# Routing turns moved from TensorE to VectorE, and routing products gathered into seven visits

## The reference

```python
h = einsum('bsd,bdh->bsh', x, W[cat]) + b[cat][:, None, :]      # 4096 x 512
probs = softmax(h @ Wr, axis=-1)                                # 8 experts
eidx = argmax(probs, axis=-1); p_tok = probs[eidx]
rank = cumsum(onehot(eidx)) - onehot(eidx)   # place in the expert's queue
keep = rank < 512                            # capacity 4096 / 8
xe = h[dispatch]                             # 8 x 512 x 512
ye = relu(xe @ W1) @ W2                      # hidden width 2048
out = x + scatter(ye * p_tok * keep)
```

## Time and profile before

| | us |
|---|---|
| median of three runs | 802.54 |
| lowest and highest | 802.49, 803.22 |
| span of the profiled execution (first to last instruction) | 800.5 |
| TensorE busy in it | 792.1 (99%) |
| VectorE busy | 576.6 (72%) |
| GpSimd busy | 512.8 (64%) |
| ScalarE busy | 351.4 (44%) |
| granted TensorE clock, mean | 0.999 of full |

### The profile page before, as it was taken

How to read it: one execution, slowest core, us unless ns; L and a number is a source line. 1 busy time by engine, 2 the same in 40 slices (tenths; PEclk the granted TensorE clock), 3 DMA queues, 4 the chain that set the end, 5 groups by cost and what they waited for, 6 DMA issues and landing times.

```text
span 800.5 us, 14226 instructions
## 1 busy us (share of the span) xinstructions
PE 792.1 (99%) x5267; PEld 704.0 (88%) x5267; DVE 576.6 (72%) x760; ACT 351.4 (44%) x537; POOL 512.8 (64%) x392
## 2 busy tenths in 40 slices
PE   9999999999999999999999999999999999999997
PEld 6788889899999999999999999999999999999996
DVE  5677878778767896589657965786578866895532
ACT  4322337445444544445444644464445444554430
POOL 1000148866888688787887688768876888663601
PEclk9999999999999999999999999999999999999999
DMA  8987545541544255524543454435541544255201
GB/s 279 371 300 274 226 128 183 184 134 59 189 160 145 103 180 174 170 105 170 166 155 130 161 167 144 157 102 171 176 146 55 194 152 155 104 183 178 71 1 53
DMA packets 61102, 127.20 MB, mean 159 GB/s; under 512 B 8310, under 2 KB 8310, under 8 KB 60562
## 3 DMA queue, kind: packets, MB, share of 16 engines
q1 hardware_dynamic: 47714, 95.19, 34.2%
q0 software_dynamic: 13216, 31.38, 12.1%
q10 hardware_dynamic: 144, 0.26, 0.1%
HBM read 110.13 MB, written 25.17 MB: 169 GB/s over the span
## 4 chain that ended last, share of the span: by engine, by line
PE 94%; DVE 3%; issue 1%; DMA 1%; ACT 1%; POOL 1%; POOLq 0%; ACTq 0%
PE y_ps L1502 44%; PE acc_ps L1403 20%; PE tp_ps L1403 19%; PE acc_ps L1311 5%; PE tp_ps L1311 2%; PE tp_ps L1237 1%; PE acc_ps L1329 1%; DMA early_rows<-h_rows,tok_all 1%; PE acc_ps L1295 1%; PE y_ps L1217 0%; POOL early_rows L532 0%; DVE x_split L1044 0%; DVE w_split L949 0%; DVE rows L863 0%; DVE first_x_sums L1048 0%
## 5 line engine op out<-in xcount | busy, mean ns | idle before, releaser
L1502 PE MATMUL y_ps<-w_split,xt_split 128*128 128x512 f32 x1536 | 371.2, 391 | 0.8 <-issue 0.8
L1502 PEld LDWEIGHTS y_ps<-w_split,xt_split 128*128 128x128 f32 x1536 | 280.7, 188 | 54.3 <-issue 1.0
L1403 PE MATMUL acc_ps<-x_split,w_split 128*128 128x256 f32 x1320 | 180.9, 283 | 0.8 <-DVE w_split L949 0.8
L960 DVE TENSOR_TENSOR w_split<-stage,w_split 128x1024 fp32r<-128x1024 f32 x64 | 115.7, 1846 | 90.6 <-ACT w_split L669 90.6
L1403 PEld LDWEIGHTS acc_ps<-x_split,w_split 128*128 128x128 f32 x1320 | 172.0, 191 | 5.7 <-DVE w_split L949 1.0
L1403 PE MATMUL tp_ps<-x_split,w_split 128*128 128x256 f32 x1284 | 176.3, 283 | 0.0
L1403 PEld LDWEIGHTS tp_ps<-x_split,w_split 128*128 128x128 f32 x1284 | 167.7, 191 | 4.7
L546 POOL DMA_INDIRECT rows<-h_rows,idx_all x112 | 130.8, 1168 | 32.9 <-issue 32.6
L662 ACT ACTIVATE w_split<-stage 128x1024 fp32r<-128x1024 f32 x64 | 54.0, 843 | 85.3 <-PE tp_ps L1403 41.6
L503 POOL TENSOR_TENSOR w_sums<-stage 128x512 f32<-128x512 f32 x31 | 42.5, 1371 | 71.8 <-DVE w_split L949 65.9
L949 DVE TENSOR_TENSOR w_split<-w_sums,w_split 128x1024 fp32r<-128x1024 f32 x62 | 75.5, 1220 | 5.8 <-ACT w_split L662 5.7
(11 more groups left out here) (186 smaller groups left out, 807.9 us busy)
## 6 DMA issues: line engine op xcount, KB each, us to landing
stage<-w SPq DMA_DIRECT2D x64, 1024.0 KB
b_rows<-x SPq DMA_DIRECT2D x8, 1024.0 KB
h_rows<-rows POOLq DMA_DIRECT2D x6, 1024.0 KB, 9.7
stage<-cond_wt SPq DMA_DIRECT2D x4, 1024.0 KB
x_more<-x_t SPq DMA_DIRECT2D x4, 1024.0 KB, 9.7
stage<-x_t SPq DMA_DIRECT2D x3, 1024.0 KB
stage<-cond_w SPq DMA_DIRECT2D x3, 1024.0 KB
h_rows<-rows SPq DMA_DIRECT2D x8, 256.0 KB, 2.0
```

The source lines that it names most:

```text
L960: nc.vector.tensor_tensor(w2s[:, slot, LO, ks, :], stage[:, 2 + slot, ks, :], w2s[:, slot, HI, ks, :].bitcast(f32), ALU.subtract).then_inc ...
L1403: last = nc.tensor.matmul(out, w1s[wg][:, w, wb, k, f], xes[xg][:, a, xb, k, :], start=start and k == 0 and (w, a) == (HI, HI), stop=True, ...
L1502: last = nc.tensor.matmul(y_ps[:, s, :], hts[:, (q % 2) * QF + jj, a, s * P:(s + 1) * P], w2s[:, q % 2, w, jj, :], start=(first and jj == ...
```

## The change

Two of the turns leave TensorE. `copy_m` becomes a VectorE transpose from `m_rows` to `m32`, and `choose` begins with a VectorE transpose from `logits_t` to a new tile `by_tok`, and reads that instead of PSUM. VectorE's transpose turns blocks of 32x32 where they lie, so the products now take their columns in another order (`group_of`: column group g takes tokens 32g to 32g + 31 of each 128). `m_sum`, `by_token` and their two semaphores are gone.

The lists are changed for the steps of batches 0, 1, 2 and 3 (after tile n):

| step | before | now |
|---|---|---|
| M_TURN | 4, 8, 13, 18 | the same |
| M_SUM | 5, 10, 13, 18 | 5, 9, 14, 19 |
| ROUTE | 6, 11, 15, 20 | 8, 13, 18, 20 |
| CHOOSE | 8, 13, 18, 23 | 10, 15, 20, 23 |
| PLACE | 10, 15, 20, 25 | 12, 17, 22, 25 |
| FILL | 13, 18, 23, 27 | the same |

The visits now are n = 4, 8, 13, 18, 20, 23, 27. In three of them (8, 13, 18) `m_turn` of one batch and `route` of the batch before stand in one visit. SyncE issues the weight of batch 2 ahead of chunk 4, and chunks 6 and 7 after the weights of batch 3.

```diff
-    ROUTE = [6, 11, 15, 20]
...
-    PLACE = [10, 15, 20, 25]
+    ROUTE = [8, 13, 18, 20]
...
+    PLACE = [12, 17, 22, 25]
...
+        by_tok = sb("by_tok", [P, TPB, G], f32)
...
+            load_cond(2)
             load_next_xt(4)
-            load_cond(2)
             load_next_xt(5)
             sp.wait_ge(s_turn, 2)
             load_cond_wt(2)
-            load_next_xt(6)
-            load_next_xt(7)
             load_cond(3)
             sp.wait_ge(s_turn, 3)
             load_cond_wt(3)
+            load_next_xt(6)
+            load_next_xt(7)
...
             def copy_m(b):
-                dve.wait_ge(s_m, b + 1)
+                dve.wait_ge(s_turnc, b + 1)
...
-                nc.vector.tensor_copy(m32[:, b % 2, :, :].rearrange("p k g -> p (k g)"), m_ps).then_inc(s_mcopy, 1)
+                nc.vector.transpose(m32[:, b % 2, :, :].rearrange("p k g -> p (k g)"), m_rows[:, :]
+                                    ).then_inc(s_mcopy, 1)
...
             def choose(b):
 
-                dve.wait_ge(s_lg, b + 1)
-                then(nc.vector.tensor_reduce(top[:, :], tok_ps, AX.X, ALU.max))
+                dve.wait_ge(s_ltc, b + 1)
+                nc.vector.transpose(by_tok[:, :, :].rearrange("p t g -> p (t g)"),
+                                    logits_t[:, :, :].rearrange("p c n -> p (c n)")).then_inc(s_lgt, 1)
+                dve.wait_ge(s_lgt, b + 1)
+                then(nc.vector.tensor_reduce(top[:, :], tok_logits, AX.X, ALU.max))
...
+            def group_of(columns, g):
+                return columns.rearrange("p (t a i) -> p a t i", t=NQ, a=NQ)[:, g, :, :]
...
-                                                stage[:, 0, k, g * P:(g + 1) * P], start=(k == 0), stop=(k == DK - 1))
+                                                group_of(stage[:, 0, k, :], g), start=(k == 0), stop=(k == DK - 1))
...
-            def m_sum(b):
-
-                pe.wait_ge(s_turnc, b + 1)
-                nc.tensor.transpose(m_ps, m_rows[:, :], ident[:, :]).then_inc(s_m, 1)
...
-                                                    x_in[c % 4][:, k, g * P:(g + 1) * P],
+                                                    group_of(x_in[c % 4][:, k, :], g),
...
-            def by_token(b):
-                pe.wait_ge(s_ltc, b + 1)
-                if b >= 1:
-                    pe.wait_ge(s_oh, b)
-                for c in range(CPB):
-                    last = nc.tensor.transpose(turned_ps[:, c, :], logits_t[:, c, :], ident[:, :])
-                last.then_inc(s_lg, 1)
```

More of the change, by code:

```diff
@@ L50, in moe_kernel @@
     M_TURN = [4, 8, 13, 18]
-    M_SUM = [5, 10, 13, 18]
-    ROUTE = [6, 11, 15, 20]
-    CHOOSE = [8, 13, 18, 23]
-    PLACE = [10, 15, 20, 25]
+    M_SUM = [5, 9, 14, 19]
+    ROUTE = [8, 13, 18, 20]
+    CHOOSE = [10, 15, 20, 23]
+    PLACE = [12, 17, 22, 25]
     FILL = [13, 18, 23, 27]
@@ L197, in moe_kernel @@
         table_ps = y_ps[:, 3, 0:SB * E * Q].rearrange("p (s e q) -> p s e q", s=SB, e=E)
-        turned_ps = y_ps[:, 1, 0:CPB * P].rearrange("p (c n) -> p c n", c=CPB)
-        tok_ps = y_ps[:, 1, 0:CPB * P].rearrange("p (t g) -> p t g", t=TPB)[:, :, 0:E]
         rank_ps = y_ps[:, 2, 0:TPB * E]
@@ L202, in moe_kernel @@
         idx_ps = tp_ps[:, 0, 2 * P:2 * P + NQ * E * SB].rearrange("p (q e s) -> p q e s", q=NQ, e=E)
-        m_ps = y_ps[:, 3, 0:P]
         bias_ps = y_ps[:, 3, P:P + BATCH]
@@ L206, in moe_kernel @@
         logits_ps = tp_ps[:, 0, 0:CPB * P]
+        tok_logits = by_tok[:, :, 0:E]
         held = [logits_t[:, :, :].rearrange("p c n -> p (c n)"), m32[:, :, :, :].rearrange("p b k g -> p (b k g)")]
@@ L221, in moe_kernel @@
         s_turnc = sem("m_turned_copied")
-        s_m = sem("m_product_done")
         s_mcopy = sem("m_copied")
@@ L230, in moe_kernel @@
         s_ltc = sem("logits_t_copied")
-        s_lg = sem("logits_done")
+        s_lgt = sem("logits_turned")
         s_diff = sem("diff_done")
@@ L638, in copy_turned @@
                 if b >= 1:
-                    act.wait_ge(s_m, b)
+                    act.wait_ge(s_mcopy, b)
                 nc.scalar.activation(m_rows[:, :], turn_ps, ACTF.Copy).then_inc(s_turnc, 1)
@@ L644, in copy_logits @@
                 act.wait_ge(s_lt, CPB * (b + 1))
+                if b >= 1:
+                    act.wait_ge(s_lgt, b)
                 nc.scalar.activation(logits_t[:, :, :].rearrange("p c n -> p (c n)"), logits_ps, ACTF.Identity,
@@ L876, in choose @@
                 chained[0] += 1
-                nc.vector.tensor_tensor(diff[:, :, :], tok_ps, wide(top[:, :]), ALU.subtract
+                nc.vector.tensor_tensor(diff[:, :, :], tok_logits, wide(top[:, :]), ALU.subtract
                                         ).then_inc(s_diff, 1)
@@ L1341, in _ @@
                     m_turn(M_TURN.index(n))
-                if n in CHOOSE:
-                    by_token(CHOOSE.index(n))
                 if n in FILL:
                     fill_table(FILL.index(n))
-                if n in M_SUM:
-                    m_sum(M_SUM.index(n))
                 if n in PLACE:
```

## The result

The changed kernel takes 807.74 us (median of five runs, 807.30 to 809.63) against 802.54 us (802.16 to 803.22, five runs). The ratio is 1.0068, with a 95% interval of 1.0057 to 1.0079: it is slower by 5.2 us. The forecast was 808.1 us. The span went from 800.5 to 806.0 us. All comparisons in this text leave out one execution of the experiment all_early, which took 2670.95 us beside ten of 800.68 to 801.37.

The account below looks back on a forecast made before the run. TensorE bounds the kernel, with VectorE about equally late before fill_table(3). Its start comes 0.68 + 4.36 + 0.57 = 5.61 us later, so 802.54 + 5.6 = 808.1 us; 8-in-10 range 806.2 to 810.2.

Parts of the forecast that it names:

- The new wait: place one tile ahead of fill_table makes TensorE wait 1.22, 1.43 and 2.2 us at fill_table 0 to 2.
- What TensorE is spared, with the first two waits: Up to tile 22's end: 1.97 us spared against waits of 1.22 and 1.43, so 0.68 us later.
- From tile 22 to T: VectorE's stretch from tile 22's store to fill_table(3): place(2) adds 4.36 us and the transpose 0.57.
- T: Time at which fill_table(3) can start: 101.28 us before, forecast about 106.9; everything behind follows at the same distances.
- Loads: SyncE's new order: m_turn(1)'s weight might land late, between nothing and 2.2 us; taken as nothing.
- the waits don't come: Rival: TensorE keeps the 1.97 us it is spared in the first stage, 800.6 us; chance 0.04.
- VectorE's time is absorbed: Rival of about no change: place(2)'s added time is absorbed before T, 803.2 us; chance 0.05.
- The columns in four runs: Rival: m_turn and route products reading columns in four runs of 32 are slower, around 817 us; chance 0.04.
- The clock's fall: Rival: clock drops to 1.2 GHz behind the last wait, 2.7 to 5.4 us more, 810.8 to 813.5; chance 0.05.

Follow-up runs that it names:

- all_early: Changed kernel with CHOOSE and PLACE at their tiles of before, M_SUM [5, 9, 13, 18], ROUTE as changed: 801.05 us, ratio 0.9981 to the kernel before.
- place2_early: Changed kernel with CHOOSE and PLACE of batch 2 at tiles 18 and 20, M_SUM of batch 3 at 18: 803.19 us.
- kept_warm: Changed kernel with 5, 5, 9 and 9 unneeded products ahead of the four fill_table steps, filling TensorE's waits: 807.58 us.
- turns_only: Changed kernel with the four lists and the load order of before; VectorE does the turns, ten visits: 801.30 us.
- changed_again: The changed kernel once more, nothing altered, run beside two other kernels on their chip: 807.68 us.
- four_more: Changed kernel with four more comparisons in place(0) alone, repeating what the next eight write: 810.31 us.
- turns_w1_late: turns_only with two low parts of the first expert's weight moved from tiles 23 and 24 to 28 and 29: 800.51 us.
- lists_only: Kernel before with the lists and load order of the change; TensorE does the turns, seven visits: 808.43 us.
- loads_as_before: Changed kernel with only SyncE's load order put back: 809.13 us (four runs, 807.33 to 811.25).
- place01_early: Changed kernel with CHOOSE and PLACE of batches 0 and 1 at 8, 13 and 10, 15, M_SUM of batch 2 at 13: 805.30 us.

## Why the prediction was right

**The new wait: right.** Forecast 1.22, 1.43 and 2.2 us at `fill_table` 0 to 2 and 0.5 at tile 24; measured 1.20, 1.26, 2.14 and 0.46. The length of `place` and its store was read before from one instance, and in the changed kernel all four show it: `place` takes 4.28 or 4.29 us.

**What TensorE is spared, with the first two waits: sign right, size half.** Tile 22's end was to come 0.68 us later. Counted from the start of tile 4 (17.96 before, 18.34 after), the store of tile 22 comes at 68.69 against 68.35, 0.34 later. The wait at `fill_table(1)` was put 0.17 too high. And the forecast missed that one group of products with 32 weight columns takes less when another such group follows it: `fill_table` to `route` is 53.15 - 52.69 = 0.46 us and not 0.56. That is about 0.1 at each such place, of which there are three. These corrections together are 0.5 against the 0.34 that is needed, so the other savings were put some 0.15 too high; which of them, no run tells.

**From tile 22 to T: right.** Forecast 4.36 + 0.57, measured 4.28 + 0.47. The 4.36 took off too little for the hand-over to TensorE; in the kernel before, too, VectorE goes from the start of `place(3)` to its next store in 4.28 us. The transpose of 128x256 was taken at the rate of the row of 128x512; it came out between the two ends, and its step is 0.1 shorter. place2_early shows the term of `place(2)` by itself: 4.55 us in the medians, 4.17 in T from tile 4. One reading was wrong without an effect on the sum: the 0.85 us of idle time lies ahead of the stretch from 86.3 to 101.3 us. The 1.34 that VectorE is idle within it are the wait of 0.75 for ScalarE and gaps between instructions.

**The start.** Tile 4 starts 0.38 us later in the changed profile. No step that the change touches lies ahead of it, and in the other profiles its start lies anywhere from 17.93 to 18.59, so this is most likely the execution and not the change. So the span's 5.5 us are 0.38 + 0.34 + 4.75, and the good agreement of 5.6 with 5.5 owes 0.4 to chance; without the start the profiles give 5.1, and the timed medians say 5.2.

**Loads: taken at nothing, right for the changed kernel, and the reason was incomplete.** No load was late in it. But the new order mattered: without it the median is 1.4 us higher (809.13 against 807.7), and 1.8 in the schedule of kept_warm. The sentence that SyncE's order "takes two loads out of the way of those needed sooner" was the mechanism, as far as two profiles show it, and what it is worth was not worked out: with the old order the change would have cost 6.7 us (809.13 against 802.45).

**The rivals.** That the waits don't come, or that VectorE's time is absorbed, is refuted by the profile and by place2_early. The columns in four runs cost nothing (turns_only). The clock's fall was given 0.05 and a price of 2.7 to 5.4 us. It does happen, but behind the wait of 2.14 us at `fill_table(2)`, where VectorE was late by more and it cost nothing. The rival had placed it behind the last wait, where nothing would hide it; no profile shows a fall there, and in changed_again the clock stayed at 1.00 behind 2.19 us. The nearest case that was paid is four_more at `fill_table(0)`: 1.5 us, below the lower of the rival's two prices.

## What to carry to other kernels

Work that leaves the bounding engine is worth what is left after the engine that it goes to, and after every step that is moved along with it. Before moving a step in a list, count its length against the work between it and whoever waits for it: here a block of 4.28 us and a store stood one tile of 2.8 us ahead of its reader, and the three moves cost 6.7 us against a gain of about 1.4. They were not needed for it: all_early has the seven visits and the VectorE turns with `choose` and `place` where they were. Where an engine has next to no idle time in a stretch that another engine waits for, look for work in it that nobody needs yet: two low parts moved by five tiles brought the last 1.2 us (0.8 in turns_w1_late).

## What was not expected of the hardware

- The granted clock fell to 1.2 GHz behind waits of TensorE of 1.92 us (lists_only), 2.14 (changed, four_more, loads_as_before), 2.15 (place01_early) and 2.75 (four_more). It stayed up behind all waits up to 1.27 us, and in changed_again, another execution of the changed kernel, behind waits of 2.13 and 2.19. It was low for about 3.5 us in the changed kernel (92.5 to 96) and for at least 3 in four_more (54 to 57).
- From the start of a group with 32 weight columns to the start of the next group takes about 0.1 us less where that one has 32 weight columns too: `m_turn` to `route` is 34.53 - 33.63 = 0.90 us in the changed kernel, `m_turn` to the 128-wide turns was 1.01 before.
- VectorE's transpose of 128x256 in f32 takes 435 ns from SBUF, 128x128 300 ns, while that of 128x512 with strided columns takes 1090; a straight line through the first two would give about 705. Whether it is the stride that costs the rest no run tells. In the groups by line of the changed kernel:

```profile
L1071 DVE STREAM_TRANSPOSE turned<-rows 128x512 f32<-128x512 f32 x28 | 28.9, 1090 | 0.0
L874 DVE STREAM_TRANSPOSE by_tok<-logits_t 128x256 f32<-128x256 f32 x4 | 1.7, 435 | 0.0
L853 DVE STREAM_TRANSPOSE m<-m_rows 128x128 f32<-128x128 f32 x4 | 1.2, 300 | 0.0
```
